# Three of eight groups of the second feed-forward product by seven quarter products, in turn with plain groups, and the residuals in two buffers

## The chip, the cores and the metric

The kernel runs on 1 core of one Trainium2 chip. The metric is the time of one execution in device microseconds, lower is better. Before the change it is 487.46 us, the median of 3 runs (487.34 to 488.05).

## The reference

The input x has 2 batches of 2048 tokens with 512 features. A recurrence `h = tanh(x @ Wx + b + h @ Wh)` runs over the tokens; its states go through a feed-forward block in which activations, weights and biases are rounded to integers times a scale, and x is added at the end:

```python
h = jax.nn.relu(quant_linear(states, w1, b1))   # 512 -> 2048 features
x = x + quant_linear(h, w2, b2)                 # 2048 -> 512 features
```

`quant_linear` divides its activations by one scale for the whole tensor (largest value / 255), rounds and clips them to 0..255, and rounds the weights to -128..127 with a scale for each output feature. The scale of the hidden activations is thus known only when all of the first product is done.

## The kernel before, in words

There are 4096 tokens, in 8 groups of GTOK = 512. Features lie on the 128 partitions: the 512 inputs and outputs are KT = 4 tiles, the 2048 hidden features are FT = 16 tiles, which are handled in pairs (f, f+1).

**Stages.** The input product x @ Wx with the recurrence's first guesses (to about 125 us), the recurrence itself (to about 239 us), corrections, the first feed-forward product of all eight groups (L823, to 366 us), a short stretch in which the largest hidden value is found (L946, L950), and the second feed-forward product (L958, from 370.5 us to the end). The input product is itself made by seven quarter products out of eight (p1 to p7, L711 to L757, with sums on POOL, L577 to L586). Only the second feed-forward product changes.

**Where the hidden values lie.** The first product leaves f32 values in SBUF. Four areas `keep[:, 0]` to `keep[:, 3]` hold a group each; groups 5, 6 and 7 (SPILLED) are written to HBM during the first product and fetched again, in four 1 MB pieces each, into the areas of groups 0, 1 and 2 once those are used; group 4 (LAST) has twelve tiles in `last_keep`, at the start of the arena, and its tiles 8 to 11 (HELD) stay in the PSUM banks 0 to 3.

**The second product before.** PE runs `second_products(g)` for g = 0 to 7 (L995 to L1005): 16 hidden tiles times 4 output tiles are 64 matmuls of 512 columns, which add up in the banks 4 to 7. The matmuls read the integers (16-bit patterns read as f16) from a ring `hidden`/`hq` of HQ_RING = 8 tiles. The pairs f = 0, 4, 8, 12 (OWN) are made by DVE (`hidden_pair`, L1761), the pairs 2, 6, 10, 14 by ACT (`relus`, L1281), each as one instruction of 1024 elements; each waits for `hq_used`, that is for PE to have used the pair that lay in the same two slots, four pairs earlier. For the last three hidden tiles PE finishes one output tile after another (`last_products`, L982), so that the outputs come staggered.

**The output.** The residual x is loaded into `xb` (4 tiles of 512 f32, one buffer), POOL adds the bias b2 to it (L596), DVE multiplies the PSUM tile by its scale and adds it into `xb` (`output`, L1757; the fourth tile goes by ACT L1307 and DVE L1750), and SP stores it (L535). DVE makes the outputs of group g-1 between its hidden pairs of group g, ACT the fourth tile between its pairs. SP's list for each group: store four tiles, load the next residual (it waits for the stores), fetch two pieces of a spilled group.

Each engine runs its list strictly in the order written in the program; an instruction that waits holds all behind it. The order around the change is thus the one that the code writes out for each engine:

```python
def hidden_group(g, source, fetches=None):        # DVE, before
    for f in OWN:
        if f == 4:
            output(g - 1, range(KT - 1))
        if f == 8:
            output(g - 1, range(KT - 1, KT))
```

Of the kernel before, what the change touches and what calls it, by code (L numbers as in the profile page):

```python
# [97 lines left out]
def tokens(g):  # L98

    return TOKENS[g]  # L100
# [12 lines left out]
SECOND_UNCHECKED = 2  # L113
FIRST_BANK = (0, 1, 2, 3, 0, 1, 6, 4, 5, 2, 3, 0, 1, 6, 4, 5)
# [51 lines left out]
def rnn_ffn_program(nc, xT, h0T, wx, wh, bT, w1, b1T, w2, b2T, ident, yT):  # L166
    with ExitStack() as ctx:
# [49 lines left out]
        def error_of(t):  # L217
# [27 lines left out]
        xb = part(last_tiles * GTOK, KT * GTOK).rearrange("p (k t) -> p k t", k=KT)  # L245
# [15 lines left out]
            "p (i f) -> p i f", i=KT)  # L261

# [140 lines left out]
        own_ready = sem("own_ready")  # L403
        hq_used = sem("hq_used")
# [3 lines left out]
        xb_landed = [sem(f"xb_landed{k}") for k in range(KT)]  # L408
# [48 lines left out]
        def _(sp):  # L457
# [61 lines left out]
            def fetch(s, quarters):  # L519

                sp.wait_ge(relu_ready, (s + 1) * (PAIRS - len(OWN)))
                sp.wait_ge(own_ready, (s + 1) * len(OWN))
                for n in quarters:

                    sp.wait_ge(spilled[n], 16 * SPILL)
                    if s > 0:
                        sp.wait_ge(fetched[n], 16 * s)
                    at = PLACE[SPILLED[s]] * keep_words + n * piece
                    nc.sync.dma_start(keep_flat[:, at:at + piece],
                                      spill[s, :, n * piece:(n + 1) * piece]).then_inc(fetched[n], 16)  # L530

            def store(g):
                for d in range(KT):
                    sp.wait_ge(y_ready, Y_RING + g * KT + d + 1)
                    nc.sync.dma_start(yT_v[tokens(g), d], xb[:, d]).then_inc(y_stored[d], 16)  # L535

            def load_again(g):

                for d in range(KT):
                    sp.wait_ge(y_stored[d], g * 16)  # L540
                    nc.sync.dma_start(xb[:, d], xTk_v[tokens(g), d]).then_inc(xb_landed[d], 16)
# [3 lines left out]
            for d in range(KT):  # L545
                nc.sync.dma_start(xb[:, d], xTk_v[tokens(0), d]).then_inc(xb_landed[d], 16)
            for g in range(2 * SPILL):
                store(g)
                load_again(g + 1)
                fetch(g // 2, (0, 1) if g % 2 == 0 else (2, 3))  # L550
            store(GROUPS - 2)
            load_again(GROUPS - 1)
            store(GROUPS - 1)
# [5 lines left out]
        def _(pool):  # L559
# [32 lines left out]
            with pool.Fori(0, GROUPS) as g:  # L592
                for d in range(KT):
                    pool.wait_ge(xb_landed[d], g * 16 + 16)
                    pool.sem_inc(xb_begun, 1)
                    nc.gpsimd.tensor_scalar(xb[:, d], xb[:, d], bq2[:, d:d + 1], None,  # L596
                                            ALU.add).then_inc(xb_ready, 1)
# [3 lines left out]
        def _(pe):  # L601
# [211 lines left out]
            def keep_going(n, at=IDLE_BANK):  # L813
                idle_products(n, at, w1t[:, 0, 0:P], w1t[:, 0, 0:GTOK])
# [154 lines left out]
            def opening_products(g):  # L969

                for f in range(2):
                    wait_hidden(g, f)
                    for d in range(KT - 1):
                        if f == 0:

                            pe.wait_ge(y_ready, g * KT + d + 1)
# [27 lines left out]
            with pe.Fori(0, GROUPS) as g:  # L1004
                second_products(g)  # L1005
# [3 lines left out]
        def _(act):  # L1009
# [271 lines left out]
            def relus(g, source, fetches=None, first=False):  # L1281

                for f in range(0, FT, 2):
                    if f == 4 and not first:
                        scale_output(g - 1)
                    if f in OWN:
                        continue
                    if fetches is not None:
                        act.wait_ge(fetched[f * QUARTERS // FT], fetches * 16)
                    act.wait_ge(hq_used, g * FT + f + 2)  # L1290
                    if source is None and f in HELD:
                        for e in range(2):
                            made = nc.scalar.activation(
                                hidden[:, (f + e) % HQ_RING, :], bank[:, (f + e) % 8, :], ACT.Relu,
                                bias=bias1[:, f + e:f + e + 1], scale=scale1[:, f + e:f + e + 1])
                    else:
                        src = last_pair(f) if source is None else source(f)
                        made = nc.scalar.activation(hidden[:, f % HQ_RING:f % HQ_RING + 2, :], src,  # L1298
                                                    ACT.Relu, scale=s_hid_inv[:, 0:1])
                    made.then_inc(relu_ready, 1)  # L1300

            def scale_output(g):

                d = KT - 1
                act.wait_ge(hq_used, HQ_RING + g * FT + FT)
                act.wait_ge(y_ready, Y_RING + g * KT)
# [3 lines left out]
            relus(0, lambda f: keep[:, 0, f:f + 2, :], first=True)  # L1310
            act.wait_ge(scales2_ready, 1)
            with act.Fori(1, LAST) as g:
                relus(g, lambda f: keep[:, g, f:f + 2, :])
            relus(LAST, None)
            with act.Fori(SPILLED[0], GROUPS) as g:
                relus(g, lambda f: keep[:, g - SPILLED[0], f:f + 2, :],
                      fetches=g - (SPILLED[0] - 1))
# [3 lines left out]
        def _(dve):  # L1321
# [422 lines left out]
            def output(g, tiles, last=False):  # L1744
                for d in tiles:
                    dve.wait_ge(xb_ready, g * KT + d + 1)
                    if d == KT - 1 and not last:

                        dve.wait_ge(y_half, 1 + g + 1)
                        nc.vector.tensor_tensor(xb[:, d], y_scaled[:, :], xb[:, d],  # L1750
                                                ALU.add).then_inc(y_ready, 1)
                        continue
                    if d < KT - 1:
                        dve.wait_ge(y_acc, g * (KT - 1) + d + 1)
                    else:
                        dve.wait_ge(hq_used, HQ_RING + g * FT + FT)
                    nc.vector.scalar_tensor_tensor(  # L1757
                        out=xb[:, d], in0=bank[:, 4 + d, :], scalar=s2_bits[:, d:d + 1],
                        in1=xb[:, d], op0=ALU.mult, op1=ALU.add).then_inc(y_ready, 1)

            def hidden_pair(g, f, source):  # L1761
                dve.wait_ge(hq_used, g * FT + f + 2)
# [4 lines left out]
            def held_pair(g, f):  # L1767

                for e in range(2):
                    nc.vector.tensor_scalar(u_own[:, e, :], bank[:, (f + e) % 8, :],  # L1770
                                            scale1[:, f + e:f + e + 1], bias1[:, f + e:f + e + 1],
                                            ALU.mult, ALU.add).then_inc(own_rounded, 1)
                dve.wait_ge(own_rounded, 2)
                dve.wait_ge(hq_used, g * FT + f + 2)
# [71 lines left out]
```

## Time and profile before

| | |
|---|---|
| median of 3 runs | 487.46 us (487.34 to 488.05) |
| the profiled execution | 487.62 us, span 485.5 us |
| PE busy (matmul) | 473.8 us, 98% of the span |
| DVE, ACT, POOL busy | 300.8, 235.8, 94.8 us |
| second product: first to last matmul start | 370.5 to 480.8 us |

The span is the time from the first to the last instruction of the profiled execution; 2.1 us lie around it. A matmul's record also holds its way through the array, so records overlap: the rate is read from starts, not from the mean duration. Idle time of an engine matters only where PE, which is nearly always busy, waits for it.

### The profile page before, as it was taken

The numbers are of one execution on the slowest core, as the hardware profiler recorded it, in microseconds if no ns is written. First come the engines' busy times: TensorE is split into PE (matmuls) and PEld (weight loads), VectorE is DVE, ScalarE is ACT, GpSimd is POOL, SyncE is SP. The second block draws the span as 40 slices with busy tenths as digits, with TensorE's granted clock in tenths as the row PEclk, the third lists the DMA queues.
The fourth block names the chain that finished last, engine by engine and source line by source line (L and its number), as shares of the span: only waits on it lengthen the run. The fifth ranks groups of instructions, "written<-read, shape, count | busy, mean of one in ns | idle before, by whom it ended". The sixth has DMA issues, their size and how long they took to land.

```text
span 485.5 us, 8663 instructions
## 1 busy us (share of the span) xinstructions
PE 473.8 (98%) x3000; PEld 324.4 (67%) x3000; DVE 300.8 (62%) x491; ACT 235.8 (49%) x452; POOL 94.8 (20%) x69
## 2 busy tenths in 40 slices
PE   8998999999999999999989999999999999999996
PEld 3687888888999999999865444444443444444442
DVE  2799856368345454454688899978777443344442
ACT  0326454554233333232489888888865333333330
POOL 2843180300000000000000000000001355544344
PEclk9999999999999999999999999999999999999999
DMA  8974422200349000000000277700002389888882
GB/s 291 387 280 173 175 88 86 81 8 1 76 97 173 0 1 0 0 0 0 1 3 0 92 322 292 319 20 0 0 0 88 103 308 306 316 305 277 291 326 103
DMA packets 38168, 65.41 MB, mean 135 GB/s; under 512 B 19056, under 2 KB 19200, under 8 KB 34560
## 3 DMA queue, kind: packets, MB, share of 16 engines
q1 hardware_dynamic: 37472, 64.04, 38.2%
q10 hardware_dynamic: 576, 1.05, 0.7%
q8 instruction: 13, 0.21, 0.2%
q14 instruction: 11, 0.09, 0.1%
q0 software_dynamic: 96, 0.01, 0.0%
HBM read 39.93 MB, written 20.97 MB: 125 GB/s over the span
## 4 chain that ended last, share of the span: by engine, by line
PE 90%; DVE 6%; ACT 1%; issue 1%; DMA 1%; DVEq 0%; ACTq 0%
PE bank L958 22%; PE bank L823 21%; PE bank L620 14%; PE bank L657 12%; PE bank L663 12%; PE bank L647 3%; PE bank L705 3%; PE bank L683 1%; DVE arena L1345 1%; DVE w_absmax L1338 1%; DMA arena<-x_t 1%; ACT arena L1157 1%; DVE slot_max L1504 1%; DVE arena L1498 0%; ACT arena L1163 0%
## 5 line engine op out<-in xcount | busy, mean ns | idle before, releaser
L596 POOL TENSOR_SCALAR arena<-arena,bq 128x512 f32<-128x512 f32 x32 | 54.1, 1705 | 327.3 <-DVEq L1800 275.8
L823 PE MATMUL bank<-arena,w_words 128*128 128x512 f16 (+1 forms) x512 | 112.3, 379 | 0.0
L958 PE MATMUL bank<-arena,w2t 128*128 128x512 f16 x512 | 110.7, 379 | 0.5 <-DVE arena L1763 0.5
L1163 ACT ACTIVATE arena<-bank,bq,s_bits 128x512 f32<-128x512 f32 (+1 forms) x126 | 90.2, 767 | 21.1 <-PE bank L823 15.4
L958 PEld LDWEIGHTS bank<-arena,w2t 128*128 128x128 f16 x512 | 49.7, 98 | 61.5 <-DVE arena L1757 2.0
L823 PEld LDWEIGHTS bank<-arena,w_words 128*128 128x128 f16 x512 | 49.6, 98 | 57.9
L1716 DVE TENSOR_REDUCE hid_parts<-arena 128x1 f32<-128x1024 f32 x60 | 70.6, 1212 | 12.6 <-ACT arena L1163 12.3
L657 PE MATMUL bank<-arena 128*128 x512 | 63.5, 277 | 0.0
L663 PE MATMUL bank<-arena 128*128 x512 | 62.4, 275 | 0.0
L657 PEld LDWEIGHTS bank<-arena 128*128 128x128 f32 x512 | 59.7, 192 | 0.6 <-issue 0.4
L663 PEld LDWEIGHTS bank<-arena 128*128 128x128 f32 x512 | 59.7, 192 | 0.0
L1298 ACT ACTIVATE arena<-arena,s_hid_inv 128x1024 uint16 (+1 forms) x31 | 35.4, 1145 | 47.8 <-PE bank L958 47.2
L620 PE MATMUL bank<-arena,w_words 128*128 128x256 f32 x224 | 53.4, 383 | 1.2 <-DVE arena L1394 1.2
L1763 DVE TENSOR_SCALAR arena<-arena,s_hid_inv 128x1024 uint16 (+1 forms) x31 | 25.1, 811 | 39.9 <-PE bank L958 39.7
L1453 DVE TENSOR_TENSOR bank<-bank,arena 128x128 f32<-128x128 f32 x80 | 24.0, 300 | 35.7 <-PE bank L663 26.9
L1131 ACT ACTIVATE arena<-bank 128x128 f32 (+1 forms) x80 | 22.3, 278 | 49.0 <-DVE bank L1453 46.4
L620 PEld LDWEIGHTS bank<-arena,w_words 128*128 128x128 f32 x224 | 41.5, 190 | 6.7 <-DVE arena L1394 1.6
L620 PE MATMUL bank<-arena 128*128 128x256 f32 x168 | 40.2, 381 | 0.0
L1026 ACT ACTIVATE arena<-bank,b_sb 128x256 f32<-128x256 f32 x56 | 23.4, 468 | 29.9 <-PE bank L620 29.9
L620 PEld LDWEIGHTS bank<-arena 128*128 128x128 f32 x168 | 31.3, 190 | 4.4 <-issue 0.4
L1394 DVE TENSOR_TENSOR arena<-bank,arena 128x512 f32<-128x512 f32 x21 | 14.3, 690 | 27.0 <-PE bank L620 26.5
L1757 DVE SCALAR_TENSOR_TENSOR arena<-bank,s_bits,arena 128x512 f32<-128x512 f32 x25 | 17.3, 746 | 22.0 <-PE bank L958 21.8
(110 smaller groups left out, 358.7 us busy)
## 6 DMA issues: line engine op xcount, KB each, us to landing
spill<-arena SPq DMA_DIRECT2D x12, 1024.0 KB, 3.9
arena<-spill SPq DMA_DIRECT2D x12, 1024.0 KB, 8.6
arena<-w SPq DMA_DIRECT2D x8, 1024.0 KB, 5.1
arena<-x_t SPq DMA_DIRECT2D x32, 256.0 KB, 3.7
y_t<-arena SPq DMA_DIRECT2D x32, 256.0 KB, 2.3
arena<-x_t SPq DMA_DIRECT2D x7, 1024.0 KB, 8.5
arena<-x_t ACTq DMA_DIRECT2D x4, 256.0 KB, 5.8
arena<-wx SPq DMA_DIRECT2D x4, 256.0 KB, 5.3
```

Source lines behind the costliest of these rows:

```text
L596: nc.gpsimd.tensor_scalar(xb[:, d], xb[:, d], bq2[:, d:d + 1], None, ALU.add).then_inc(xb_ready, 1)
L620: mm = nc.tensor.matmul(bank[:, at, j * HALF:(j + 1) * HALF], weights[:, k, j * P:(j + 1) * P], x_half[:, k, :], start=(first and j == 0 a ...
L657: nc.tensor.matmul(bank[:, at + j, 0:COLS], wh_sb[:, k, j * P:(j + 1) * P], state(k), start=(k == 0), stop=False)
L663: mm = nc.tensor.matmul(bank[:, at + j, 0:COLS], wh_sb[:, k, j * P:(j + 1) * P], state(k), start=False, stop=(k == KT - 1))
L823: return nc.tensor.matmul(bank[:, at, :], w1t[:, k, f * P:(f + 1) * P], states_in[:, k, :], start=(k == 0), stop=(k == KT - 1))
L958: return nc.tensor.matmul(bank[:, 4 + d, :], w2t[:, f, d * P:(d + 1) * P], hq[:, f % HQ_RING, :], start=(f == 0), stop=(f == FT - 1))
L1026: nc.scalar.activation(out[:, :, j, :], bank[:, chain_bank(i), j * HALF:(j + 1) * HALF].rearrange("p (s c) -> p s c", c=COLS), ACT.Identit ...
L1163: return nc.scalar.activation(out[:, cols], bank[:, at, cols], ACT.Identity, bias=bq1[:, f:f + 1], scale=s1_bits[:, f:f + 1])
L1298: made = nc.scalar.activation(hidden[:, f % HQ_RING:f % HQ_RING + 2, :], src, ACT.Relu, scale=s_hid_inv[:, 0:1])
L1453: nc.vector.tensor_tensor(z, z, xw[:, s, j, :], ALU.add).then_inc(sum_ready, 1)
L1716: nc.vector.tensor_reduce(hid_parts[:, columns:columns + 1], source, AX_XY, ALU.max).then_inc(kept_seen, 1)
L1763: nc.vector.tensor_scalar(hidden[:, f % HQ_RING:f % HQ_RING + 2, :], source, s_hid_inv[:, :], 0.0, ALU.mult, ALU.max).then_inc(own_ready, 1)
```

## The change

The groups are taken in the order 4, 3, 0, 5, 1, 6, 2, 7. Those at the places 2, 4 and 6 (the groups 0, 1 and 2, which lie in SBUF) go by quarters: hidden tiles are halved (8 and 8), tokens are halved (256 and 256), output tiles are halved (2 and 2), and seven products of such quarters take the place of eight. One quarter product is 8 x 2 matmuls of 256 columns. It needs four sums of the w2 quarters (`w2_sum`, made once, in the place of w1) and four of the hidden quarters (`whole_sum`, for each such group), all on DVE. The hidden integers of such a group are all made by ACT (`whole_pairs`), in place of the f32 values, before its products start. The partial results are added into the residual by DVE after each product (`take`), so the quarter products use only the banks 0 to 2, and `take` goes into two output tiles, of 256 columns each, one instruction for each.

The other five groups (places 0, 1, 3, 5, 7) go as before through the ring. The residual has two buffers in turn, so that a load no longer waits for the store of the group just before it. The spilled pieces are fetched to other places and in other numbers: 2, 3, 3, 2, 2 pieces at the groups 0 to 4. The loops over groups are written out instead of being loops of the chip. The two idle-matmul operands move from w1 to w2, since w1's place is overwritten.

```diff
+ORDER = (LAST, 3, 0, 5, 1, 6, 2, 7)
+BY_QUARTERS = (2, 4, 6)
+PLAIN = (0, 1, 3, 5, 7)
+CHAIN_BANK, PLAIN_BANK, OTHER_BANK = 0, 1, 2
+TAKEN = 5
...
 # SP
+            load_again(0)
+            sp.wait_ge(relu_ready, 1)
+            sp.wait_ge(own_ready, 1)
+            load_again(1)
+            fetches = {0: (0, 1), 1: (2, 3, 4), 2: (5, 6, 7), 3: (8, 9), 4: (10, 11)}
+            for n in range(GROUPS):
+                if n == 0:
+                    for k in fetches[0]:
+                        fetch(k)
+                store(n)
+                if n + 2 < GROUPS:
+                    load_again(n + 2)
+                for k in fetches.get(n, ()) if n > 0 else ():
+                    fetch(k)
...
 # PE
+            def quarter_product(at, weights, hidden_quarter, first=False):
+                for f in range(HALF_F):
+                    for j in range(2):
+                        mm = nc.tensor.matmul(bank[:, at, j * HALF:(j + 1) * HALF],
+                                              weights[:, f, j * P:(j + 1) * P], hidden_quarter[:, f, :],
+                                              start=(first and f == 0 and j == 0),
+                                              stop=(f == HALF_F - 1), skip_group_check=True)
+                mm.then_inc(quarter_made, 1)
+
+            def products_by_quarters(i):
+                g = ORDER[BY_QUARTERS[i]]
+                pe.wait_ge(whole_made, (i + 1) * PAIRS)
+                if i > 0:
+                    pe.wait_ge(y_ready, Y_RING + (BY_QUARTERS[i - 1] + 1) * KT)
+                quarter_product(CHAIN_BANK, w2_part(0, 0), whole_part(g, 0, 0), first=True)
+                quarter_product(PLAIN_BANK, w2_part(1, 0), whole_part(g, 1, 0), first=True)
+                pe.wait_ge(w2_sums, 2)
+                pe.wait_ge(whole_sums, 4 * i + 3)
+                pe.wait_ge(quarter_taken, TAKEN * i + 1)
+                quarter_product(CHAIN_BANK, w2_sum(1), whole_sum(g, 2))
+                quarter_product(OTHER_BANK, w2_sum(0), whole_sum(g, 1), first=True)
+                pe.wait_ge(w2_sums, 4)
+                pe.wait_ge(quarter_taken, TAKEN * i + 3)
+                quarter_product(CHAIN_BANK, w2_sum(2), whole_sum(g, 3))
+                pe.wait_ge(quarter_taken, TAKEN * i + 4)
+                quarter_product(OTHER_BANK, w2_sum(3), whole_part(g, 1, 1))
+                pe.wait_ge(whole_sums, 4 * i + 4)
+                pe.wait_ge(quarter_taken, TAKEN * i + 5)
+                quarter_product(CHAIN_BANK, w2_part(1, 1), whole_sum(g, 4))
...
 # ACT
+            def whole_pairs(i, first, end):
+                g = ORDER[BY_QUARTERS[i]]
+                for pair in range(first, end):
+                    if pair > 0:
+                        act.wait_ge(whole_made, i * PAIRS + pair)
+                    nc.scalar.activation(whole_ints(g, pair), keep[:, g, 2 * pair:2 * pair + 2, :],
+                                         ACT.Relu, scale=s_hid_inv[:, 0:1]).then_inc(whole_made, 1)
...
+            ring_pair(0, 2)
+            ring_pair(0, 6)
+            whole_pairs(0, 0, 2)
             act.wait_ge(scales2_ready, 1)
+            ring_pair(0, 10)
+            whole_pairs(0, 2, 4)
+            ring_pair(0, 14)
+            whole_pairs(0, 4, 6)
+            ring_pair(1, 2)
+            scale_output(0)
+            ring_pair(1, 6)
+            whole_pairs(0, 6, 8)
+            ring_pair(1, 10)
+            ring_pair(1, 14)
+            for i in range(len(BY_QUARTERS)):
+                ring_pair(i + 2, 2)
+                scale_output(i + 1)
+                ring_pair(i + 2, 6)
+                if i + 1 < len(BY_QUARTERS):
+                    whole_pairs(i + 1, 0, 6)
+                    ring_pair(i + 2, 10)
+                    whole_pairs(i + 1, 6, 8)
+                else:
+                    ring_pair(i + 2, 10)
+                ring_pair(i + 2, 14)
...
 # DVE
+            def sums_of_whole(i):
+                g = ORDER[BY_QUARTERS[i]]
+                dve.wait_ge(whole_made, (i + 1) * PAIRS)
+                def difference(m, a, b):
+                    nc.vector.tensor_tensor(whole_sum(g, m), a, b, ALU.subtract).then_inc(whole_sums, 1)
+                difference(1, whole_part(g, 0, 1), whole_part(g, 0, 0))
+                difference(3, whole_part(g, 1, 1), whole_part(g, 0, 1))
+                dve.wait_ge(whole_sums, 4 * i + 1)
+                difference(2, whole_part(g, 1, 1), whole_sum(g, 1))
+                dve.wait_ge(whole_sums, 4 * i + 3)
+                difference(4, whole_part(g, 1, 0), whole_sum(g, 2))
+
+            def take(i, made, r, t, at, done):
+                n = BY_QUARTERS[i]
+                dve.wait_ge(quarter_made, 7 * i + made)
...
+                for j in range(2):
+                    d = 2 * r + j
+                    dve.wait_ge(xb_ready, n * KT + d + 1)
+                    block = xb(n)[:, d, t * HALF:(t + 1) * HALF]
+                    added = nc.vector.scalar_tensor_tensor(
+                        out=block, in0=bank[:, at, j * HALF:(j + 1) * HALF],
+                        scalar=s2_bits[:, d:d + 1], in1=block, op0=ALU.mult, op1=ALU.add)
...
+            ring_pair(0, OWN[2])
+            w2_sum_made(0, w2_part(0, 1), w2_part(1, 1), ALU.add)
+            ring_pair(0, OWN[3])
+            w2_sum_made(1, w2_sum(0), w2_part(0, 0), ALU.subtract)
+            ring_pair(1, OWN[0])
+            output(0, range(KT - 1))
+            ring_pair(1, OWN[1])
+            output(0, range(KT - 1, KT))
+            ring_pair(1, OWN[2])
+            w2_sum_made(2, w2_part(0, 0), w2_part(0, 1), ALU.subtract)
+            w2_sum_made(3, w2_part(1, 0), w2_sum(1), ALU.subtract)
+            ring_pair(1, OWN[3])
+            sums_of_whole(0)
+            for i in range(len(BY_QUARTERS)):
+                output(i + 1, range(KT))
+                take(i, 1, 0, 0, CHAIN_BANK, quarter_taken)
+                take(i, 2, 0, 0, PLAIN_BANK, quarter_taken)
+                ring_pair(i + 2, OWN[0])
+                take(i, 3, 0, 1, CHAIN_BANK, quarter_taken)
+                take(i, 4, 1, 1, OTHER_BANK, quarter_taken)
+                ring_pair(i + 2, OWN[1])
+                take(i, 5, 1, 1, CHAIN_BANK, quarter_taken)
+                take(i, 6, 0, 1, OTHER_BANK, y_ready)
+                take(i, 7, 1, 0, CHAIN_BANK, y_ready)
+                ring_pair(i + 2, OWN[2])
+                if i + 1 < len(BY_QUARTERS):
+                    sums_of_whole(i + 1)
+                ring_pair(i + 2, OWN[3])
+            output(len(PLAIN) - 1, range(KT), last=True)
```

`ring_pair(i, f)` makes the pair f of the i-th plain group in the ring, as `relus` and `hidden_pair` did. `whole_part(g, c, t)` is the quarter of the hidden integers with the tiles of half c and the tokens of half t, 8 x 256 16-bit elements on each partition. Each instruction of `sums_of_whole` and of `w2_sum_made` reads two such quarters and writes one.

## Rows read from the trace of the kernel before

**Rows 1.** The page: busy time, chain that ended last.

```profile
PE 473.8 (98%) x3000; PEld 324.4 (67%) x3000; DVE 300.8 (62%) x491; ACT 235.8 (49%) x452; POOL 94.8 (20%) x69
...
PE 90%; DVE 6%; ACT 1%; issue 1%; DMA 1%; DVEq 0%; ACTq 0%
```

**Rows 2.** L958, the second product: durations (min/median/max), first and last start, its waits.

```profile
L958 PE MATMUL bank<-arena,w2t x512: 379/379/389, 370.5 to 480.8; 128*128 128x512 f16 x171
...
PEld bank L958 <- DVE arena L1757: 2.0, 7, 0.3
```

**Rows 3.** Busy time in windows: group 1 (stretch, PE, PEld, DVE, ACT, POOL, clock, DMA).

```profile
384.28:398.08 13.80, 13.80 (x65) 6.22 (x64) 5.67 (x9) 5.17 (x5) 7.17 (x4) 1.00 0.89 303
```

**Rows 4.** Timeline (start, length): matmuls of 256 and 126 columns; their weight loads by line.

```profile
238.74 0.60 PE L818 MATMUL bank<-w_words 128*128 128x256 f16 x4
240.10 1.05 PE L683 MATMUL bank<-arena 128*128 128x126 f16 x16 [0.76 <-ACT bank L1150]
...
L818 PE MATMUL bank<-w_words 128*128 128x256 f16 x4 | 0.6, 272 | 0.0
...
L683 PEld LDWEIGHTS bank<-arena 128*128 128x128 f16 x192 | 10.8, 97 | 7.0 <-issue 6.0 <-ACT bank L1150 1.0
```

**Rows 5.** Timeline of the first pairs and of group 1: hidden pairs, outputs, stores.

```profile
369.67 1.41 DVE L1763 TENSOR_SCALAR arena<-arena,s_hid_inv 128x1024 uint16<-128x1024 f32 x2
369.67 2.19 ACT L1298 ACTIVATE arena<-arena,s_hid_inv 128x1024 uint16<-128x1024 f32 x2 [0.64 <-DVE s_hid_inv L1742]
...
382.56 2.07 DVE L1757 SCALAR_TENSOR_TENSOR arena<-bank,s_bits,arena 128x512 f32<-128x512 f32 x3 [2.36 <-PE bank L958]
...
388.05 1.15 ACT L1298 ACTIVATE arena<-arena,s_hid_inv 128x1024 uint16 x1 [1.73 <-PE bank L958]
```

**Rows 6.** Hidden pairs (page: busy, mean ns, idle; by line: min/median/max ns) and outputs.

```profile
L1763 DVE TENSOR_SCALAR arena<-arena,s_hid_inv 128x1024 uint16 (+1 forms) x31 | 25.1, 811 | 39.9 <-PE bank L958 39.7
...
L1763 DVE TENSOR_SCALAR arena<-arena,s_hid_inv x31: 742/753/1206, 369.7 to 472.7; 128x1024 uint16 x24, 128x1024 uint16<-128x1024 f32 x7
...
L1298 ACT ACTIVATE arena<-arena,s_hid_inv x31: 1132/1147/1151, 369.7 to 474.4; 128x1024 uint16 x24, 128x1024 uint16<-128x1024 f32 x7
...
L1757 DVE SCALAR_TENSOR_TENSOR arena<-bank,s_bits,arena x25: 740/743/752, 382.6 to 481.7; 128x512 f32<-128x512 f32 x25
```

**Rows 7.** DVE groups by shape: tensor with tensor, and one tensor, f32 and f16.

```profile
L1498 DVE TENSOR_TENSOR arena<-arena 128x252 f16<-128x252 f32 x24 | 9.0, 418 | 3.5 <-ACT arena L1157 3.5
L1354 DVE TENSOR_SCALAR arena<-arena 128x2048 f16<-128x2048 f32 x4 | 4.9, 1227 | 0.1
L1750 DVE TENSOR_TENSOR arena<-arena 128x512 f32<-128x512 f32 x7 | 4.8, 692 | 0.1
L1388 DVE TENSOR_SCALAR arena<-arena 128x2048 f16<-128x2048 f16 x1 | 0.7, 694 | 0.0
```

**Rows 8.** POOL's bias additions, and a hidden pair of DVE that fell beside one.

```profile
L596 POOL TENSOR_SCALAR arena<-arena,bq x32: 1559/1566/2114, 373.9 to 477.9; 128x512 f32<-128x512 f32 x32
...
445.05 6.45 POOL L596 TENSOR_SCALAR arena<-arena,bq 128x512 f32<-128x512 f32 x4 [6.57 <-DMA arena<-x_t]
445.08 1.21 DVE L1763 TENSOR_SCALAR arena<-arena,s_hid_inv 128x1024 uint16 x1 [2.70 <-PE bank L958]
```

**Rows 9.** Timeline: SP's stores, loads and fetches after group 1, then POOL.

```profile
397.15 3.02 SPq L535 DMA_DIRECT2D y_t<-arena  x4
400.22 2.54 SPq L541 DMA_DIRECT2D arena<-x_t  x4
402.89 0.83 SPq L529 DMA_DIRECT2D arena<-spill  x2
404.31 6.61 POOL L596 TENSOR_SCALAR arena<-arena,bq 128x512 f32<-128x512 f32 x4 [7.31 <-DMA arena<-x_t]
```

**Rows 10.** PE: matmuls of 512 columns after the start, and after a short pause at 367 us.

```profile
L610 PE MATMUL bank<-arena 128*128 128x512 bf16 x7 | 3.1, 624 | 1.4 <-DVE arena L1327 1.4
L610 PE MATMUL bank<-w_words 128*128 128x512 f16 x8 | 2.2, 381 | 0.5 <-ACT arena L1163 0.5
```

More of the change, by code:

```diff
@@ L532, in store, with fetch @@
-            def store(g):
+            def fetch(k):
+                s, n = k // QUARTERS, k % QUARTERS
+                if k < 2:
+                    sp.wait_ge(relu_ready, PAIRS - len(OWN))
+                    sp.wait_ge(own_ready, len(OWN))
+                elif k < 2 + QUARTERS:
+                    sp.wait_ge(relu_ready, 2 * (PAIRS - len(OWN)))
+                    sp.wait_ge(own_ready, 2 * len(OWN))
+                else:
+                    sp.wait_ge(quarter_made, 7 if k < 2 + 2 * QUARTERS else 14)
+                sp.wait_ge(spilled[n], 16 * SPILL)
+                if s > 0:
+                    sp.wait_ge(fetched[n], 16 * s)
+                nc.sync.dma_start(part(places[k], quarter_words),
+                                  spill[s, :, n * piece:(n + 1) * piece]).then_inc(fetched[n], 16)
@@ L1279, in _ @@
             act.wait_ge(scales1_ready, 1)
[L1281 to L1300, printed above, removed]
@@ L1302, in scale_output, with hidden_source, ring_pair @@
-            def scale_output(g):
+            def hidden_source(g, f):
+                if g == LAST:
+                    return last_pair(f)
+                return fetched_pair(g, f) if g in SPILLED else keep[:, g, f:f + 2, :]
+            def ring_pair(i, f):
+                g = ORDER[PLAIN[i]]
+                if g in SPILLED:
+                    act.wait_ge(fetched[f // QUARTERS], (SPILLED.index(g) + 1) * 16)
+                act.wait_ge(hq_used, i * FT + f + 2)
+                if g == LAST and f in HELD:
+                    for e in range(2):
+                        made = nc.scalar.activation(
+                            hidden[:, (f + e) % HQ_RING, :], bank[:, (f + e) % 8, :], ACT.Relu,
+                            bias=bias1[:, f + e:f + e + 1], scale=scale1[:, f + e:f + e + 1])
+                else:
+                    made = nc.scalar.activation(hidden[:, f % HQ_RING:f % HQ_RING + 2, :],
+                                                hidden_source(g, f), ACT.Relu,
+                                                scale=s_hid_inv[:, 0:1])
+                made.then_inc(relu_ready, 1)
@@ L1778, in hidden_group @@
-            def hidden_group(g, source, fetches=None):
-                for f in OWN:
-                    if f == 4:
-                        output(g - 1, range(KT - 1))
-                    if f == 8:
-                        output(g - 1, range(KT - 1, KT))
-                    if fetches is not None:
-                        dve.wait_ge(fetched[f * QUARTERS // FT], fetches * 16)
-                    if source is None and f in HELD:
-                        held_pair(g, f)
-                    else:
-                        hidden_pair(g, f, last_pair(f) if source is None else source(f))
```

171 lines of the change are left out of this document (98 added, 73 removed).

## The prediction

> **What bounds the kernel now.** I read the page first: PE is busy for 98% of the span, and it is 90% of the chain that ended last [rows 1]. Then the one stage that changes. Its 512 matmuls start from 370.5 to 480.8 us [rows 2], (480.8 - 370.5) / 511 = 0.216 us apart. A group of 64 is 13.82 us, a hidden tile (four matmuls) 0.864 us. There is no room between them: the table by window has PE busy for 13.80 of 13.80 us at a granted clock of 1.00, while DVE works 5.7, ACT 5.2 and POOL 7.2 us [rows 3], and the waits for outputs, 2.0 us over seven group borders, are weight loads that wait, hidden under the matmul in flight [rows 2]. So PE's work sets the end: less of it is a gain as far as DVE, ACT and POOL deliver in time.
>
> **What PE saves.** A quarter group is 7 x 16 = 112 matmuls of 256 columns in place of 64 of 512. Four such in a row took 0.60 us, the last one alone 0.272: (0.60 - 0.272) / 3 = 0.109 us apart [rows 4]. Sixteen are 1.75 us, seven products 12.24 us, so a group saves 13.82 - 12.24 = 1.58 us and three save **4.7 us**. The weight loads don't hinder: one lasts 0.097 us, yet 16 matmuls of 126 columns, each with its own load, took 1.05 us, (1.05 - 0.218) / 15 = 0.055 us apart (0.218 is one such matmul's record, estimated as 0.272 less the 130 missing columns at 0.109 / 256 us each) [rows 4].
>
> **What DVE, ACT and POOL get, and where it lies.** Four edits first.
> - *Takes.* Before, an output of 512 columns lasted 0.743 us, three in a row 2.07, so one follows the other 0.08 us before its record ends [rows 5, 6]. A fixed part of 0.15 us (below) and half the rest give 0.45 us for 256 columns, some 0.81 for the two of a take; it starts 0.2 us after its product (the first output at 382.56 follows the 55th matmul at 382.35, rows 5). The next product that needs it starts 1.75 us later. Even with a ring pair (0.75) ahead of take 5 it is done 0.6 us early. Nothing on PE; without that slack each late take would hold PE.
> - *Residuals.* POOL's additions (1.57 us each, rows 8) are ready before the groups that need them: loads of 1 MB went out at 400.2 and POOL could begin at 404.3 [rows 9]; with two buffers this comes in time, with some 5 us to go in the quarter groups. They hid before and gain nothing.
> - *Fetches.* Two pieces go out at 380 us instead of 389. The next three go out near 403; at the 303 GB/s of rows 3, 1 MB takes 3.4 us, so behind the residual they land at 408, 412 and 415. The first of them is wanted at 412, the second at 418. Nothing, with 4 us to spare; one late would hold the ring.
> - *w2 sums, and the whole pairs of the first quarter group.* Four sums and eight ACT instructions of 1.15 us lie in the groups 0 and 1, where DVE and ACT are idle more than half of the time [rows 3]. I go through both lists with the bases 370.5 and 384.3: the latest ring pair is still 2 us early, and the differences for place 2 end near 395.5, before the outputs of group 1 become ready (396.4). Nothing.
>
> **The edit that costs.** At the places 3 and 5 DVE's list reads: ring pair f = 8, `sums_of_whole` for the next quarter group, ring pair f = 12. The sums wait for all eight whole pairs, and the last two of these stand on ACT's list behind ring pair f = 10, which waits for its slots. Let T be PE's start in this plain group.
> - ACT's pair f = 10 started at 388.05 where T was 384.30, at T + 3.75 [rows 5]. Two pairs without a wait took 2.19, one 1.147: one follows 1.04 after the other [rows 5, 6]. Whole pair 6 runs T + 4.8 to 5.95, pair 7 waits for it and ends at T + 7.15. DVE begins at T + 7.2.
> - A difference is one tensor with tensor over 2048 16-bit elements; no row has it. Such rows with f32 inputs: 252 elements 0.418 us, 512 elements 0.692, so 1.054 ns an element and 0.15 us fixed, 2.31 us for 2048: the upper bound. One tensor with a scalar over 2048 took 1.227 us from f32, 0.694 from f16: the lower bound [rows 7]. In the last pair 16-bit data halves what is above the fixed part, (1.227 - 0.16) / (0.694 - 0.16) = 2. I take the same halving, 0.15 + 2.16 / 2 = 1.23 us, the form being that of the first two rows and the type that of the last. The Trainium skill ("VectorE: DVE Perf Modes", the tier table) gives 1224 ns for this form in bf16; the sum by it would be the same.
> - Four of them, 0.09 us of overlap three times and one dependent step: 4.7 us, to T + 11.9. Ring pair 12 adds 0.66 and its signal 0.05: PE has it at T + 12.6. It wants it at 12 x 0.864 = T + 10.4. **A stall of 2.2 us**, in general 4x - 2.7 for a difference of x.
> - POOL. Its additions for the next group run from about T + 5 to T + 12: stores at the end of the group before, loads, then the landing, as in rows 9. Hidden pairs of DVE last 0.753 us as a rule but up to 1.21 beside POOL [rows 6, 8]; all 31 together are 25.1 - 31 x 0.753 = 1.8 us longer, spread over the ten or so that met POOL: 0.18 each, and 1.21 - 0.75 = 0.46 the one that lost most [rows 6]. A difference is 1.6 times as long and reads two tensors in SBUF, so I take 0.3 for each and 0.2 for the pair: 1.4, say 1.3 us. Bounds: 0 (outputs, one input in PSUM, stayed at 740 to 752, rows 6) and 5 x 0.46 = 2.3.
>
> So 3.5 us a stall, at two places, 7.0 us. At place 7 there are no sums, and no stall.
>
> **Sum.** 487.62 (the profiled execution; 0.16 above the median) - 4.7 + 7.0 = **489.9 us**. By the bounds: without POOL 487.3; with 2.3 us, 491.9.
>
> **A rule against the change.** POOL's additions stretched DVE's pairs by 0.46 us at most though each lasts 1.57 [rows 6, 8]. The Trainium skill ("SBUF — State Buffer", Terms, the shared port pair) says that DVE with two SBUF inputs and a reading GpSimd lock each other out for the whole instruction. By that rule as a mechanism here: three additions stand in front of differences, 3 x 1.57 = 4.7 us a place, 2 x (2.2 + 4.7) - 4.7 = +9.1, 496.7 us. The trace is against its full length.
>
> **Rivals.**
> - *Faster: the differences run as fast as one tensor with a scalar* (0.694). The stall is 4 x 0.694 - 2.7 = 0.1 us; 487.6 - 4.7 + 0.2 = 483.1, and some 485 with POOL beside it. For it: the f16 row; against it: two inputs. The point that decides is a difference of 1.27 us with all that POOL adds: there 2 x (4x - 2.7) = 4.7, and my 1.23 lies just below it, so POOL alone makes my sign.
> - *No contention:* 487.3, no change that can be measured. For it: the outputs of DVE never stretched beside POOL; against it: the hidden pairs did.
> - *16 bits bring nothing* (2.31): stalls of 6.5 us twice; and the differences for place 2 end near 401.5, so the outputs and take 1 come 3.5 us late: 487.6 - 4.7 + 13 + 3.5 = 499.4. For it: f16 output alone did not help in the 252 row (its inputs were f32).
> - *The clock falls in the stall.* PE's pauses before are 1.4 us at most. The first seven matmuls show 624 ns in 3.1 us, against 381 later after a pause of 0.5 us [rows 10]: those went at 1.2 GHz, half of 2.4. If such a stretch follows each stall, it costs half of 3.1 us twice: 493.0.
> - *The change does not do what it says*, if 256 columns take over half as long as 512: at 0.123 us a matmul (13.82 / 112) nothing is saved, and 494.6 us is left. Rows 4 speak against it.
>
> **How the numbers follow.** The forecast, differences of about 1.23 us stretched by POOL, 488.6 to 491.9: 0.50. No contention or nearly, 486.6 to 488.4: 0.20. Fast differences or a shorter way than I see: 0.12. Clock: 0.07. Lock for whole instructions: 0.04. Slow differences: 0.04. Others, longer: 0.03. The range takes in the first two, the clock and the upper part of the third: 486.4 to 493.4, some 0.18 left out. A measurement of this kernel can tell 0.2%, 1.0 us, from no change. Slower by more: 0.48 + 0.02 (of the second) + 0.18 = 0.68. Within it: 0.02 + 0.11 = 0.13. Faster: 0.07 + 0.12 = 0.19.
>
> **What would show it.** In the waits of the changed kernel: PE for the DVE hidden pair, two times about 3.5 us, in the plain groups at the places 3 and 5 ahead of hidden tile 12, while DVE's differences (2048 16-bit elements) stand just before that pair. Quarter groups of 12.2 us without a wait in them; the differences at 1.23 us apart from POOL, 1.5 beside it; granted clock 1.00. The forecast is wrong if a difference lasts under 1 us or over 2, if PE waits for a take, for the differences of its own group or for a fetched piece, or if matmuls of 256 columns are not 0.109 us apart.

## The result, and the profile after

The changed kernel takes 491.39 us (median of 4 runs, 491.10 to 491.78), beside 487.75 us of the kernel before (4 runs, 487.34 to 488.95): a ratio of 1.007, 95% interval 1.0057 to 1.0082. It is slower by 3.6 us. The range of the prediction, 486.4 to 493.4, holds it; its 489.9 us is 1.5 us too low. The profiled execution is 491.43 us with a span of 489.6 us.

The page of the changed kernel, the same parts as in [rows 1], with the slices of the granted clock:

```profile
PE 472.5 (97%) x3144; PEld 339.3 (69%) x3144; DVE 322.7 (66%) x525; ACT 246.6 (50%) x461; POOL 99.1 (20%) x69
...
PEclk9999999999999999999999999999999999899899
...
PE 86%; DVE 8%; ACT 3%; issue 2%; DMA 1%; DVEq 0%; ACTq 0%
```

PE is busy for 1.3 us less than before, in a span 4.1 us longer. In the chain that ended last, 4 points have gone from PE to DVE and ACT, and in two places the clock slices read 8 where all were 9. The waits of the changed kernel, from 366 us on (who waited for whom: us in total, times, longest), say who came late:

```profile
DVE arena L1915 <- ACT arena L1401: 8.7, 2, 4.4
PEld bank L1017 <- DVE arena L1900: 7.1, 2, 3.8
PE bank L1017 <- DVE arena L1900: 6.7, 3, 3.3
```

L1017 is the plain group's matmul, L1900 DVE's ring pair, L1915 a difference, L1401 a whole pair, L1067 a quarter product's matmul. DVE stands twice for ACT's whole pairs, and PE twice for the ring pair behind the differences. (The third PE wait is the stage's start, as before.) No take makes PE wait.

The timeline of the plain group at place 3 shows the chain; PE begins it at T = 410.40 (each row: start, length, engine, line, operation, how many, and in brackets how long the engine had been idle and what ended that):

```profile
410.40 10.52 PE L1017 MATMUL bank<-arena,w2t 128*128 128x512 f16 x48
...
414.12 1.15 ACT L1390 ACTIVATE arena<-arena,s_hid_inv 128x1024 uint16<-128x1024 f32 x1 [7.07 <-PE bank L1017]
415.17 2.31 ACT L1401 ACTIVATE arena<-arena,s_hid_inv 128x1024 uint16<-128x1024 f32 x2
416.69 1.98 SPq L595 DMA_DIRECT2D arena<-x_t  x4
417.52 5.04 DVE L1915 TENSOR_TENSOR arena<-arena 128x2048 f16<-128x2048 f16 x4 [4.36 <-ACT arena L1401]
...
419.70 7.50 POOL L655 TENSOR_SCALAR arena<-arena,bq 128x512 f32<-128x512 f32 x4 [9.26 <-DMA arena<-x_t]
...
422.49 1.17 DVE L1900 TENSOR_SCALAR arena<-arena,s_hid_inv 128x1024 uint16<-128x1024 f32 x1
...
423.72 5.31 PE L1017 MATMUL bank<-arena,w2t 128*128 128x512 f16 x16 [2.79 <-DVE arena L1900]
```

ACT's pair f = 10 runs at T + 3.7, the two whole pairs behind it end at T + 7.1, DVE's four differences run to T + 12.2, its pair f = 12 to T + 13.3, and PE, which wanted that pair at 420.75, goes on at 423.72. Then PE itself is slow: 16 matmuls take until 428.87, 5.15 us for 3.45 us of work. The windows say why (stretch: length, busy PE, PEld, DVE, ACT, POOL, granted clock, DMA share, GB/s); the first three are place 3, the next two place 5, the last a quarter group:

```profile
410.40:420.75 10.35, 10.35 (x50) 4.61 (x47) 4.86 (x6) 4.49 (x4) 1.09 (x2) 1.00 0.89 311
420.75:423.72 2.97, 0.18 (x2) 0.01 (x1) 2.88 (x3) 1.15 (x1) 2.97 (x2) 1.00 0.93 300
423.72:428.87 5.15, 5.15 (x17) 1.97 (x17) 1.78 (x3) 0.00 (x0) 3.49 (x3) 0.67 1.01 424
...
451.45:454.90 3.45, 0.17 (x1) 0.00 (x0) 3.36 (x3) 1.15 (x1) 3.45 (x3) 0.97 0.94 384
454.90:459.92 5.02, 5.02 (x16) 1.97 (x17) 1.74 (x3) 0.00 (x0) 1.95 (x2) 0.68 0.30 124
398.18:410.40 12.22, 12.22 (x113) 10.96 (x112) 7.66 (x16) 8.50 (x8) 6.93 (x5) 1.00 0.94 326
```

After each wait the granted clock falls to 0.67 or 0.68 of 2.4 GHz on the mean of the stretch, that is, most of it ran at 1.2 GHz. The quarter groups last 12.22, 12.23 and 12.23 us (starts at 398.18, 428.87 and 459.92, PE's next group at 410.40, 441.10 and 472.15).

The bill, against the 13.82 us of a plain group: three quarter groups -4.8; waits 2.97 + 3.45 = +6.4; slow matmuls 5.15 + 5.02 - 2 x 3.45 = +3.3. That is +4.9 from the stage's start (370.5 in both traces) to its last matmul, and the spans differ by 4.1: the end behind the last matmul is 0.8 us shorter, which the sixth experiment looks at. Outside the span it is 1.8 us after against 2.1 before, so the two executions differ by 3.8 us.

### The profile page after: what moved, and what is told of

It reads as the page before. It is cut to its first block, busy times and chain, and to the rows that moved or that the text cites. A ratio compares the mean times of both kernels' runs of the same rounds, so it can differ in the third digit from the quotient of the medians.

```text
span 489.6 us, 8744 instructions
## 1 busy us (share of the span) xinstructions
PE 472.5 (97%) x3144; PEld 339.3 (69%) x3144; DVE 322.7 (66%) x525; ACT 246.6 (50%) x461; POOL 99.1 (20%) x69
## 4 chain that ended last, share of the span: by engine, by line
PE 86%; DVE 8%; ACT 3%; issue 2%; DMA 1%; DVEq 0%; ACTq 0%
PE bank L882 21%; PE bank L679 14%; PE bank L716 12%; PE bank L722 12%; PE bank L1017 12%; PE bank L1067 7%; PE bank L706 3%; PE bank L764 3%; DVE arena L1915 2%; PE bank L742 1%; DVE arena L1464 1%; DVE w_absmax L1457 1%; ACT arena L1401 1%; DMA arena<-x_t 1%; ACT arena L1250 1%
## 5 line engine op out<-in xcount | busy, mean ns | idle before, releaser
L655 POOL TENSOR_SCALAR arena<-arena,bq 128x512 f32<-128x512 f32 x32 | 58.3, 1837 | 315.6 <-DVEq L1951 275.5
L1017 PE MATMUL bank<-arena,w2t 128*128 128x512 f16 x320 | 73.3, 391 | 6.7 <-DVE arena L1900 6.7
L1017 PEld LDWEIGHTS bank<-arena,w2t 128*128 128x128 f16 x320 | 31.8, 100 | 47.1 <-DVE arena L1900 7.1
L1390 ACT ACTIVATE arena<-arena,s_hid_inv 128x1024 uint16<-128x1024 f32 x19 | 21.6, 1144 | 40.2 <-PE bank L1017 39.4
L1224 ACT ACTIVATE arena<-arena x48 | 14.9, 310 | 30.6 <-DVE arena L1565 26.6
L1565 DVE TENSOR_TENSOR arena<-bank,arena 128x128 f32 x48 | 14.0, 291 | 23.4 <-PE bank L722 22.9
```

The lines of the kernel that those rows point to most:

```text
L655: nc.gpsimd.tensor_scalar(xb(n)[:, d], xb(n)[:, d], bq2[:, d:d + 1], None, ALU.add).then_inc(xb_ready, 1)
L1017: return nc.tensor.matmul(bank[:, 4 + d, :], w2t[:, f, d * P:(d + 1) * P], hq[:, f % HQ_RING, :], start=(f == 0), stop=(f == FT - 1))
L1224: nc.scalar.activation(dst(j), src(j), ACT.Tanh).then_inc(state_ready, 1)
```

## Experiments

Where nothing else is said, an edit is made to the changed kernel, and the ratios are to the kernel before. The second product's matmuls start at 370.5 to 372.1 us in these executions: the front part, which no experiment touches, differs by up to 1.6 us from one execution to the next. Where a kernel is judged by its trace, I therefore give the stretch from the first to the last of these matmuls: 110.3 us before (370.5 to 480.8), 115.2 after (370.5 to 485.7).

**1. Ring pair 12 ahead of the differences.**

```diff
                 ring_pair(i + 2, OWN[2])
-                if i + 1 < len(BY_QUARTERS):
-                    sums_of_whole(i + 1)
                 ring_pair(i + 2, OWN[3])
+                if i + 1 < len(BY_QUARTERS):
+                    sums_of_whole(i + 1)
```

> Only DVE's order at the places 3 and 5 changes: ring pair f = 12 goes ahead of the four differences. Theory (PE waits for that pair because it is queued behind the differences, and the clock falls in the wait): both waits (2.97 and 3.45 us) and the slow stretches behind them (some 1.6 us each) go, the differences still end near T + 12.5, before anybody needs them: 491.4 - 9.7 = 481.7 us, 1.2% under the kernel before. Rival, that the pair is late because its slots or its fetched pieces are late: the waits stay, 491.4. Rival, that the differences then come late for the next quarter group: PE waits there instead, some 485 or more.

Measured: 482.32 us (481.60 to 483.15), 0.9876 of the kernel before, 0.9853 to 0.9899. Its timeline at place 3:

```profile
411.33 13.98 PE L1017 MATMUL bank<-arena,w2t 128*128 128x512 f16 x64
...
416.79 0.75 DVE L1900 TENSOR_SCALAR arena<-arena,s_hid_inv 128x1024 uint16<-128x1024 f32 x1 [2.70 <-PE bank L1017]
418.45 5.13 DVE L1915 TENSOR_TENSOR arena<-arena 128x2048 f16<-128x2048 f16 x4 [0.91 <-ACT arena L1401]
...
423.50 2.06 DVE L1877 SCALAR_TENSOR_TENSOR arena<-bank,s_bits,arena 128x512 f32<-128x512 f32 x3
```

PE runs 64 matmuls in one piece; the pair is made at T + 5.5, in the gap in which DVE stood before, and the differences run at the same place as ever (T + 7.1 to T + 12.3), where nobody needs them. First to last matmul 106.1 us, 9.1 less than in the changed kernel. A wait on DVE's list ahead of work that was ready cost 9 us, with the slow matmuls behind it, and the change is a gain once that is gone. One small wait is new:

```profile
DVE arena L1934 <- POOL arena L655: 0.9, 1, 0.9
...
PE bank L1067 <- DVE arena L1934: 0.3, 1, 0.3
```

In the last quarter group a take waited for POOL's addition, 0.9 us, and PE for the take, 0.3 us: without the two long waits, the residual is now the next thing to be late.

**2. All whole pairs ahead of ACT's ring pair 10.** DVE keeps the order of the changed kernel.

```diff
-                    whole_pairs(i + 1, 0, 6)
+                    whole_pairs(i + 1, 0, 8)
                     ring_pair(i + 2, 10)
-                    whole_pairs(i + 1, 6, 8)
```

> DVE's order stays as in the changed kernel (differences ahead of ring pair 12); ACT makes all eight whole pairs ahead of its ring pair f = 10. Theory (the differences are late only since the last two whole pairs stand behind that ring pair): whole pairs end before the plain group begins, the differences start at T + 2.8 instead of T + 7.1 and end near T + 8, ring pair 12 at T + 9, before PE's T + 10.4: no wait, 481.7 us. Rival, that DVE has too little room for them ahead of tile 12 whatever ACT does: a wait of some us stays, 485 to 491.

Measured: 483.30 us (483.00 to 485.03), 0.9913 of the kernel before, 0.9885 to 0.9941; first to last matmul 105.8 us. That median is 1.6 us above the 481.7 expected; in the profiled execution the front part is 1.0 us longer than in the changed kernel's.

```profile
411.37 13.98 PE L1017 MATMUL bank<-arena,w2t 128*128 128x512 f16 x64
...
414.04 4.75 DVE L1914 TENSOR_TENSOR arena<-arena 128x2048 f16<-128x2048 f16 x4
...
418.70 0.74 DVE L1899 TENSOR_SCALAR arena<-arena,s_hid_inv 128x1024 uint16<-128x1024 f32 x1
```

The differences now start at T + 2.7, pair 12 is done at T + 8.1. The same wait goes by an edit on another engine: it needed both the two late whole pairs on ACT and the order on DVE. The interval of this kernel reaches into that of the first; I don't tell the two apart.

**3. The wait filled with idle matmuls.**

```diff
                 for f in range(2, FT - TOGETHER):
+                    if f == OWN[3] and g in (2, 3):
+                        keep_going(12, 3)
                     wait_hidden(g, f)
```

> The changed kernel, with 12 matmuls of 512 columns into the unused bank 3 ahead of PE's wait for hidden tile 12 at the places 3 and 5 (12 x 0.216 = 2.6 us, shorter than either wait). They compute nothing that is used. Theory (the granted clock of 0.67 and 0.68 in the 5.1 us behind each wait comes of PE's idling in it): the clock stays at 1.00 and the stretches take 3.45 instead of 5.15 and 5.02 us: 491.4 - 3.2 = 488.2 us. Rival, that the clock has another cause, or that PE is slow there for want of DVE or ACT: no change, 491.4.

Measured: 488.44 us (10 runs, 487.51 to 490.19), 1.001 of the kernel before, 0.9996 to 1.0025; first to last matmul 111.5 us, 3.7 less than in the changed kernel. The windows of the filled wait and of the 16 matmuls behind it, place 3:

```profile
421.56:424.52 2.96, 2.76 (x14) 1.08 (x12) 2.87 (x3) 1.15 (x1) 2.96 (x2) 1.00 0.79 253
424.52:427.98 3.46, 3.46 (x16) 1.58 (x17) 1.67 (x3) 0.00 (x0) 3.46 (x3) 1.00 1.00 424
```

PE is released as late as ever, but the clock stays at 1.00 and the 16 matmuls take 3.46 us in place of 5.15. So the slow stretch comes of the idling; DVE and ACT did the same work beside it in both. At place 5 the 16 matmuls take 3.47 us in place of 5.02. The clock is thus worth 3.2 us of the 3.7; the other 0.5 us is a shorter wait at place 5, 2.95 us in place of 3.45, where POOL began only 1.5 us behind the differences (448.82 and 447.33) and stretched one of them in place of two.

**4. Without POOL's additions.** The bias b2 is left out of the result.

```diff
-                    nc.gpsimd.tensor_scalar(xb(n)[:, d], xb(n)[:, d], bq2[:, d:d + 1], None,
-                                            ALU.add).then_inc(xb_ready, 1)
+                    pool.sem_inc(xb_ready, 1)
```

> The changed kernel without POOL's 32 additions of the output bias b2 (POOL only passes the residuals on; b2 is left out of the result). Theory (DVE's differences and pairs are stretched by POOL beside them, from 1.226 to 1.26 and 1.38 us on the mean of four, pair 12 from 0.753 to 1.17): differences at 1.226, waits of 2.1 us each instead of 2.97 and 3.45, so 2.2 us less: 489.2 if the clock still falls, 486.0 if the shorter idling leaves it at 1.00. Rival, that POOL doesn't matter: 491.4.

Measured: 488.00 us (10 runs, 487.82 to 488.56), 1.000 of the kernel before, 0.9990 to 1.0009; first to last matmul 110.1 us (372.1 to 482.2).

```profile
412.01 10.52 PE L1016 MATMUL bank<-arena,w2t 128*128 128x512 f16 x48
...
419.13 4.75 DVE L1914 TENSOR_TENSOR arena<-arena 128x2048 f16<-128x2048 f16 x4 [4.36 <-ACT arena L1400]
...
423.80 0.75 DVE L1899 TENSOR_SCALAR arena<-arena,s_hid_inv 128x1024 uint16<-128x1024 f32 x1
...
424.60 3.63 PE L1016 MATMUL bank<-arena,w2t 128*128 128x512 f16 x16 [2.07 <-DVE arena L1899]
```

```profile
422.36:424.60 2.24, 0.17 (x1) 0.00 (x1) 2.15 (x3) 1.15 (x1) 0.00 (x0) 1.00 0.86 264
424.60:428.07 3.47, 3.47 (x17) 1.58 (x18) 1.68 (x3) 0.00 (x0) 0.00 (x0) 1.00 0.94 368
```

Alone, four differences take 4.75 us and the pair 0.75, and PE waits 2.24 us at both places (at place 5: 48 matmuls from 440.29, 10.35 us, and the next at 452.88). POOL's part of a wait is thus 2.97 - 2.24 = 0.7 us at place 3 and 3.45 - 2.24 = 1.2 us at place 5. And after 2.24 us without work the clock held at 1.00 in this execution. From first to last matmul it is 5.1 us less than in the changed kernel, as expected of the second case (2.2 + 3.2 = 5.4). The median is 2.0 us above the 486.0 of that case. In the profiled execution the front part is 1.6 us longer than in the changed kernel's, at a granted clock of 0.999 on the mean. The nine other runs took as long, 487.82 to 488.56 us, but each has a mean granted clock of 0.996, and 0.003 x 486 us is some 1.5 us of full-speed work (an estimate), about what one slow stretch cost in the changed kernel (1.7 and 1.6 us). So the clock may well have fallen behind one of the two waits in these nine; they left no trace that would show where. That it holds after 2.24 us is shown for one execution in ten.

**5. Residuals loaded only behind the stores of the group just before.** On the kernel of the first experiment.

```diff
 def load_again(n):
-                    if n > 1:
-                        sp.wait_ge(y_stored[d], (n - 1) * 16)
+                    if n > 0:
+                        sp.wait_ge(y_stored[d], n * 16)
...
-            load_again(1)
...
-                if n + 2 < GROUPS:
-                    load_again(n + 2)
+                if n + 1 < GROUPS:
+                    load_again(n + 1)
```

> On the kernel with ring pair 12 first (482.3 us): each residual is loaded only once the four stores of the group just before are done, as with one buffer; the rest, buffers and fetches, stays. My prediction gave the two buffers no part in the time. Theory (that holds only for plain groups; a quarter group takes its residual 1.8 us after its start): POOL's first two additions end some 8 us after the start of a quarter group, take 1 at + 9, while PE wants it at + 3.5: 5 to 6 us of waiting in each of three quarter groups, and 1.6 us each if the clock falls: 482.3 + 17 to 23 = 499 to 505 us. By the prediction as it stood: 482.3.

Measured: 509.55 us (2 runs, 508.94 and 510.16), 1.0445 of the kernel before, 1.0424 to 1.0466. The first quarter group, whose products begin at 399.14:

```profile
401.23 2.68 SPq L595 DMA_DIRECT2D arena<-x_t  x4
404.03 1.32 SPq L582 DMA_DIRECT2D arena<-spill  x3
405.31 6.68 POOL L654 TENSOR_SCALAR arena<-arena,bq 128x512 f32<-128x512 f32 x4 [5.43 <-DMA arena<-x_t]
406.98 0.48 DVE L1933 SCALAR_TENSOR_TENSOR arena<-bank,s_bits,arena 128x256 f32<-128x256 f32 x1 [6.15 <-POOL arena L654]
408.45 1.45 DVE L1933 SCALAR_TENSOR_TENSOR arena<-bank,s_bits,arena 128x256 f32<-128x256 f32 x3 [0.99 <-POOL arena L654]
409.08 9.08 PE L1066 MATMUL bank<-arena,w_words 128*128 128x256 f16 x64 [6.28 <-DVE arena L1933]
...
PE bank L1066 <- DVE arena L1933: 20.0, 3, 8.2
```

PE waits 20.0 us in three quarter groups, 2 us above the high end of what I expected, and the clock fell behind these waits too (0.976 on the mean of the execution): the 64 matmuls of 256 columns behind the first wait took 9.08 us in place of 7.15. The time is 4.5 us above the expected 499 to 505. Loading two groups ahead, which the second buffer allows, is worth 509.6 - 482.3 = 27 us here. In a kernel of plain groups alone the loads were hidden without it (POOL's additions made nobody wait); the quarter groups as they stand can't do without it.

**6. The kernel before with DVE's loops written out.**

```diff
-            with dve.Fori(1, LAST) as g:
+            for g in range(1, LAST):
...
-            with dve.Fori(SPILLED[0], GROUPS) as g:
+            for g in range(SPILLED[0], GROUPS):
```

> The kernel before, with only DVE's two loops over groups in the second product written out, as the changed kernel has them. In the trace the changed kernel's end (from PE's last matmul to the end of the span) is some 0.8 us shorter than before's, where DVE has 0.28 us of 'issue' ahead of the last three outputs. Theory (the loop's end costs that): the 0.28 goes, and the time is 0.3 to 0.8 us lower, 487.1 to 487.6. Rival (the end is the way the last stores land): no change, 487.9, and the 0.28 stays or goes without effect.

Measured: 487.78 us (11 runs), 0.9993 of the kernel before, 0.9983 to 1.0002. The last outputs, first in the kernel before, then in this one:

```profile
479.35 0.75 DVE L1757 SCALAR_TENSOR_TENSOR arena<-bank,s_bits,arena 128x512 f32<-128x512 f32 x1 [5.90 <-PE bank L958]
...
480.38 2.07 DVE L1757 SCALAR_TENSOR_TENSOR arena<-bank,s_bits,arena 128x512 f32<-128x512 f32 x3 [0.28 <-issue]
```

```profile
479.56 2.73 DVE L1757 SCALAR_TENSOR_TENSOR arena<-bank,s_bits,arena 128x512 f32<-128x512 f32 x4 [5.93 <-PE bank L958]
```

The gap of 0.28 us between the first and the second output is gone, and from PE's last matmul (start 480.8 and 481.0) to the end of the span it is 4.7 us before and 3.9 here: the 0.8 us by which the changed kernel's end is shorter as well. As a whole, the interval of the time reaches from a gain of 0.8 us to a loss of 0.1: consistent, not shown.

**7. Both orders.** The edits of the experiments 1 and 2 together.

> Both orders: ACT's eight whole pairs ahead of its ring pair 10, and DVE's ring pair 12 ahead of the differences. Theory: with no wait left either cure alone is worth as much as both, 482.3 (the waits seen with either alone add up to under 1 us). Rival, that the earlier differences free DVE and POOL for the residual that was 0.3 us late in the last quarter group: 482.0 or so, not to be told apart. If DVE were still a bound: more than 1 us lower.

Measured: 482.71 us (482.12 to 482.93), 0.9897, 0.9881 to 0.9912; first to last matmul 105.8 us. Not to be told from either alone, so there was one cause with two conditions.

**8. Both orders, and the fetches spread.**

```diff
-            fetches = {0: (0, 1), 1: (2, 3, 4), 2: (5, 6, 7), 3: (8, 9), 4: (10, 11)}
+            fetches = {0: (0, 1), 1: (2, 3), 2: (4, 5, 6), 3: (7, 8, 9), 4: (10, 11)}
```

> As the kernel with both orders, and the pieces are fetched 2, 2, 3, 3, 2 at the groups 0 to 4 in place of 2, 3, 3, 2, 2, so that the residual's loads and stores find the queues less full. Theory (fetches hide): POOL's additions begin 1 to 3 us earlier in the middle groups, the time stays within 0.3 us of the kernel with both orders. Rival, that a fetch comes late for a ring pair now: a wait of PE for a hidden pair in plain group 5, 1 us or more longer.

Measured: 482.45 us (481.88 to 482.80), 0.9887, 0.9872 to 0.9902: no difference that can be told, as expected. In its waits ACT stands 6.8 us for fetched pieces (1.1 us in the kernel with both orders) and PE for takes 0.6 us in all: the room that the fetches have is nearly used up. POOL's additions during place 3, first with both orders alone, then here:

```profile
420.20 7.30 POOL L655 TENSOR_SCALAR arena<-arena,bq 128x512 f32<-128x512 f32 x4 [9.57 <-DMA arena<-x_t]
```

```profile
417.09 7.88 POOL L655 TENSOR_SCALAR arena<-arena,bq 128x512 f32<-128x512 f32 x4 [6.64 <-DMA arena<-x_t]
```

With two pieces fetched before them in place of three, they begin 6.7 us after PE's start of the group in place of 9.6, and those of the next group 9.3 in place of 12.0, as expected. In the two groups after these, which were not part of the expectation, they begin 0.8 and 2.4 us later.

The kernel of the first experiment, with that one call moved, is 1.2% faster than the one before (1.0 to 1.5%).

## Why the prediction was right, and where it was off

- **What PE saves** stands: 12.22 and 12.23 us for a quarter group against the 12.24 worked out, 4.8 us in all. The first, seventh and eighth experiments leave 4.2, 4.5 and 3.9 us of it from first to last matmul; the rest are small waits for takes, by the matmuls' starts 0.9 us in the eighth.
- **The cause** stands, each link as put: the pair f = 12 behind the differences, these behind the last whole pairs, those behind the pair f = 10. Start of the differences T + 7.2 against T + 7.1 measured; one difference 1.23 against 1.226 (median of twelve); the wait without POOL 2.2 against 2.24. The rivals of fast (0.694) and of slow differences (2.31, worked out from the f32 rows) fall by that one row. The value of a difference at which the sign turns is 1.26 by the prediction's own sum, not 1.27; nothing hangs on it.
- **POOL's part** was 1.3 us at each place; measured 0.7 and 1.2. The step that failed is the start of the additions and how many of DVE's instructions they stretch. I had T + 5; they ran from T + 9.3 (419.70 - 410.40) and T + 7.2 (448.27 - 441.10). SP issued the loads only at T + 6.3 at place 3, since they wait for stores that were in the queue behind three fetched pieces: its waits for stores reach 4.6 us, where the kernel before had 0.8 at most. I had given three pieces at once no price; the eighth experiment shows it, 2.9 us of the start at place 3 for one piece more. So fewer additions fell beside the differences. I had also priced all four differences at 0.3 and the pair at 0.2; at place 3 POOL stretched the last difference (1.51 us) and the pair (1.17), at place 5, where it began with the differences, the last two (1.63 and 1.60) and the pair (1.18). The 1.2 us there is near the 1.3 I had, but as two differences at 0.4 and a pair at 0.4, and not as five small losses.
- **The clock** is what the sum lacked. I had it as a rival with a chance of 0.07 and a price of half of 3.1 us at each place; it came true at both, at 1.7 and 1.6 us. My reason against it, that PE's longest pause so far was 1.4 us, said nothing on a pause of 3.5, which I was forecasting in the same text: with a wait of that length as the likeliest case, its consequence belonged in the sum. In the profiled execution of the fourth experiment the clock held after 2.24 us without work; in the changed kernel it fell after 2.97 us.
- So the sum 487.6 - 4.7 + 7.0 = 489.9 should have been 487.6 - 4.8 + 6.4 + 3.3 = 492.5, less the 1.1 us that the loops' end and the way around the span gave back: 491.4.
- **POOL and DVE holding each other up for whole instructions**, 496.7 us, did not come. A difference beside POOL lasted up to 1.630 us, 0.40 more than alone, and the four POOL additions at place 5, beside the differences, 8.58 us, against 6.45 in [rows 8]. Both directions in one view, durations in ns (min/median/max):

```profile
L1915 DVE TENSOR_TENSOR arena<-arena x12: 1210/1226/1630, 390.4 to 452.2; 128x2048 f16<-128x2048 f16 x12
...
L655 POOL TENSOR_SCALAR arena<-arena,bq x32: 1559/1608/3648, 373.5 to 470.3; 128x512 f32<-128x512 f32 x32
```

  The Trainium skill ("SBUF — State Buffer", Terms) has the loser blocked for the other's full instruction. For POOL the trace does not speak against it: one addition took 3.65 us, 2.1 more than the 1.56 of one that nothing stretched, and a difference lasts 1.2 to 1.6. A difference lost 0.40 us at most beside additions of 1.56 and more: against it in that direction.
- **Residuals**: right that they cost nothing in the changed kernel, but the "some 5 us" of room were 1.7 at place 4 (additions end at 427.20, the group begins at 428.87) and 3.1 at place 6; the first experiment, which has no waits, used it up. "Gain nothing" was true of the plain groups only: with the loads one group later the quarter groups made PE wait 20.0 us (fifth experiment).
- **Takes, w2 sums, first quarter group**: no wait in any of them. Two instructions of a take last 0.88 us against 0.81; one of them, 256 columns, lasts 0.479 us where I had 0.45. Its fixed part is 2 x 0.479 - 0.743 = 0.22 us, where I had 0.15.

## What to carry to other kernels

A saving on the engine that sets the end is only as good as the order on the engines that feed it: go through each in-order list and ask of every new wait what ready work stands behind it, and who needs that first. Here the ring pair could be made 1.7 us before the input of the differences was there, and moving one line turned +0.7% into -1.2%. A wait of the matrix engine of some 3 us is to be priced with the clock that it loses behind it, here half as much again; a shorter one may not be safe either (2.24 us, fourth experiment).

## What the runs showed of the hardware that was not expected

- The clock held after 2.24 us without matmuls in the one execution profiled (1.00; nine others had 0.996 on the mean in place of 0.999), and fell after 2.97 us (0.67 over the next 5.15 us) and 3.45 us (0.68 over 5.02 us); idle matmuls into an unused bank held it at 1.00 (3.2 us less in the two stretches of 16 matmuls behind the waits).
- The end of a loop of the chip on DVE showed as 0.28 us of "issue" between the first and the second of the kernel's last outputs and was gone with the loop written out.
- Under DVE's back-to-back differences POOL lost more than DVE: up to 2.1 us on an addition of 1.56, against 0.40 on a difference of 1.23.
